# Converting the feed-forward weight to bf16 in 256 half-row transfers instead of 512 quarter-row ones, with a bf16 scratch tile

## The reference

```python
# attention, 16 heads of 64
q, k, v = rope(ln(x) @ wq.T), rope(ln(x) @ wk.T), ln(x) @ wv.T
scores = q k^T / 8 + slope_h * (key position - query position), causal
x = x + softmax(scores) @ v @ out_w.T + out_b
# feed-forward
xr = ln(x).reshape(b, t, 64, 16)
y = einsum('btri,hrij->bthrj', xr, rail_maker)      # 4 heads, 64 rails of 16
z = einsum('bthrj,hrkj->bthrk', y, rail_up_proj)    # 16384 columns
x = x + gelu(z.reshape(b, t, 16384)) @ w_cproj.T    # w_cproj is (1024, 16384)
```

## Time and profile before

| What | us |
|---|---|
| median of two runs | 3660.29 (3616.95 and 3703.63) |
| the profiled execution | 3630.47 |
| its span, slowest core (core 0) | 3628.9 |
| spans of the eight cores | 3590.0 to 3628.9 |
| PE busy | 2168.0 (60%) |
| ACT busy | 1058.1 (29%) |
| DVE busy | 770.3 (21%) |
| POOL busy, with its transfer issues | 372.6 (10%) |

### The profile page before, as it was taken

One profiled execution on the slowest core, in us unless ns is written; L12 is line 12 of the kernel. 1 busy time (PEld: TensorE's weight loads), 2 busy tenths in 40 slices (PEclk: granted clock), 3 DMA queues, 4 the chain that ended last, 5 costly groups with the idle time before them and its releaser, 6 DMA issues.

```text
span 3628.9 us, 34661 instructions; the slowest of 8 cores (3590.0 to 3628.9 us)
## 1 busy us (share of the span) xinstructions
PE 2168.0 (60%) x8094; PEld 862.7 (24%) x8094; DVE 770.3 (21%) x1803; ACT 1058.1 (29%) x1967; POOL 372.6 (10%) x705
## 2 busy tenths in 40 slices
PE   1268107426556665653000399759897887988989
PEld 0023002101111211211000122214343443434434
DVE  3300772224444444442000022200000000000000
ACT  1312111025445555552000011153232332333320
POOL 0022000122222222222222100000000000000000
PEclk9999557555666667675555555559998999999999
DMA  1122001353333333333333322238898888988888
GB/s 40 53 29 24 6 0 12 42 83 54 55 53 55 54 55 53 54 54 53 55 53 54 71 73 73 67 100 262 253 277 247 258 275 255 281 267 255 284 278 278
DMA packets 392162, 439.65 MB, mean 121 GB/s; under 512 B 63264, under 2 KB 247584, under 8 KB 391968
## 3 DMA queue, kind: packets, MB, share of 16 engines
q1 hardware_dynamic: 282368, 365.03, 33.5%
q0 software_dynamic: 98080, 47.23, 11.7%
q10 hardware_dynamic: 11520, 25.17, 1.8%
HBM read 425.73 MB, written 58.72 MB: 133 GB/s over the span
## 4 chain that ended last, share of the span: by engine, by line
DMA 44%; PE 33%; issue 9%; DVE 6%; ACT 4%; SPq 2%; POOL 1%; DVEq 0%; POOLq 0%; ACTq 0%
DMA wcv<-wcT 19%; PE pf L1047 17%; DMA wcb<-wcv 11%; DMA wcs<-wcb 11%; PE pat L902 6%; PE pqk L380 3%; PE pf L997 3%; PE pqk L494 2%; DMA bbuf<-blkB 2%; SPq L975 1%; DMA w2b<-w2scr 1%; DVE scrW L427 1%; SPq L991 1%; ACT sqd L254 1%; DVE lnst L248 1%
## 5 line engine op out<-in xcount | busy, mean ns | idle before, releaser
L1047 PE MATMUL pf<-wcs,Hb 128*128 128x512 bf16 x4096 | 1012.2, 385 | 156.8 <-DMA wcs<-wcb 155.1
L1010 ACT ACTIVATE Hb<-pf 128x256 bf16<-128x256 f32 x1024 | 394.4, 385 | 735.4 <-PE pf L997 710.2
L1047 PEld LDWEIGHTS pf<-wcs,Hb 128*128 128x128 bf16 x4096 | 393.9, 99 | 588.2 <-issue 230.8
L676 PE MATMUL ps<-qstg,KT 128*128 128x512 bf16 x559 | 308.7, 554 | 255.6 <-DVE qstg L668 219.6
L902 PE MATMUL pat<-owt,Ost 64*128 64x512 bf16 x512 | 224.1, 629 | 376.2 <-issue 376.2
L594 POOL DMA_DIRECT2D wcv<-wcT x512 | 271.3, 530 | 985.0 <-DMA wcb<-wcv 948.3
L753 PE MATMUL po<-pbuf,Vx 128*65 128x512 bf16 x559 | 309.5, 555 | 98.3 <-DVE Ost L812 80.5
L997 PE MATMUL pf<-btb,w2b 128*128 128x256 bf16 x1024 | 288.0, 289 | 43.6 <-DMA w2b<-w2scr 15.2
L1064 DVE TENSOR_TENSOR ob<-pf,xr 128x512 f32<-128x512 f32 x32 | 22.1, 692 | 1250.9 <-PE pf L997 891.1
L718 ACT ACTIVATE ebuf<-ps,cpool 128x512 bf16<-128x512 f32 x303 | 208.9, 689 | 88.3 <-PE ps L676 58.1
L711 ACT ACTIVATE ebuf<-ps,cpool 128x1024 bf16<-128x1024 f32 x128 | 142.9, 1116 | 281.3 <-PE ps L676 261.1
(11 more groups left out here) (99 smaller groups left out, 1335.3 us busy)
## 6 DMA issues: line engine op xcount, KB each, us to landing
wcs<-wcb SPq DMA_DIRECT2D x1024, 256.0 KB, 5.0
wcv<-wcT POOLq DMA_DIRECT2D x512, 64.0 KB, 2.6
wcb<-wcv SPq DMA_DIRECT2D x512, 64.0 KB, 1.5
w2b<-w2scr SPq DMA_DIRECT2D x256, 128.0 KB, 3.7
xin<-x SPq DMA_DIRECT2D x16, 512.0 KB, 4.2
xrb<-x SPq DMA_DIRECT2D x16, 512.0 KB, 5.1
xres<-xnw ACTq DMA_DIRECT2D x16, 512.0 KB, 5.3
xr<-xres SPq DMA_DIRECT2D x16, 512.0 KB, 6.7
```

Source lines behind the costliest of these rows:

```text
L676: P.op("tensor", (lambda p_=pr, f_=hf, kc_=kc, hc_=hc, qp_=qc % 2: (lambda e: e.matmul(ps[p_][:, 512 * f_:512 * (f_ + 1)], KT[0:128, S * h ...
L1010: P.op("scalar", (lambda m_=mc, z_=zb, p_=p: (lambda e: e.activation(Hb2[p_][:, SB2 * m_:SB2 * (m_ + 1)], pf[z_][:, 0:SB2], AF.Gelu, bias= ...
L1047: P.op("tensor", (lambda m_=mc, s_=sl2, e_=e2, pi=pb_i, i_=i, p_=p: (lambda e: e.matmul(pf[pi][:], Hb2[p_][:, SB2 * m_ + 128 * s_:SB2 * m_ ...
```

## The change

The conversion is cut in 256 rounds instead of 512. The two tiles `wcv` become [128, 512] instead of [128, 256], so a load fetches 2 KB of each of 128 rows instead of 1 KB, and a store writes 1 KB of each row instead of 512 bytes. The bytes in total, the two tiles, the two issuing engines and the waits between load and store are as before. The order of the instructions on all engines is as before too.

`sqd` becomes bf16. The sums of the exponentials stay float32 and no longer pass through it: DVE copies them straight into `rrow`, ACT's Ln works in place there, and the copy now also names `rrow_evt` among its waits.

```diff
-    sqd = es.enter_context(nc.sbuf_tensor("sqd", [128, 1024], F32))
+    sqd = es.enter_context(nc.sbuf_tensor("sqd", [128, 1024], BF16))
...
-    wcv = [p3_es.enter_context(nc.sbuf_tensor(f"wcv{i}", [128, D // 4], BF16, side="right"))
+    wcv = [p3_es.enter_context(nc.sbuf_tensor(f"wcv{i}", [128, D // 2], BF16, side="right"))
            for i in range(2)]
...
-    for mh in range(512):
-        mc, hh = divmod(mh, 4)
+    for mh in range(256):
+        mc, hh = divmod(mh, 2)
         i = mh % 2
         P.op("gpsimd", (lambda m_=mc, h_=hh, i_=i: (lambda e: e.dma_start(
-            out=wcv[i_][:], in_=wcT_d[128 * m_:128 * (m_ + 1), 256 * h_:256 * (h_ + 1)])))(),
+            out=wcv[i_][:], in_=wcT_d[128 * m_:128 * (m_ + 1), 512 * h_:512 * (h_ + 1)])))(),
              waits=[wcv_st[i]], inc=f"dcv{i}")
         wcv_ld[i] = P.now(f"dcv{i}")
         P.op("sync", (lambda m_=mc, h_=hh, i_=i: (lambda e: e.dma_start(
-            out=wcb_d[128 * m_:128 * (m_ + 1), 256 * h_:256 * (h_ + 1)], in_=wcv[i_][:])))(),
+            out=wcb_d[128 * m_:128 * (m_ + 1), 512 * h_:512 * (h_ + 1)], in_=wcv[i_][:])))(),
              waits=[wcv_ld[i]], inc=f"dcb{i}")
...
-    P.op("vector", lambda e: e.memset(sqd[64:66, :], 1.0), inc="v")
+    P.op("vector", lambda e: e.memset(rrow[64:66, :], 1.0), inc="v")
...
             P.op("vector", (lambda p_=pob: (lambda e: e.tensor_copy(
-                sqd[64:65, 512 * p_:512 * (p_ + 1)], po[p_][64:65, :])))(),
-                 waits=[ev_av, ev_vconst, drow_evt[pob]], inc="v")
+                rrow[64:65, 512 * p_:512 * (p_ + 1)], po[p_][64:65, :])))(),
+                 waits=[ev_av, ev_vconst, drow_evt[pob], rrow_evt[pob]], inc="v")
...
             rrow[64:66, 512 * p_:512 * (p_ + 1)],
-            sqd[64:66, 512 * p_:512 * (p_ + 1)],
+            rrow[64:66, 512 * p_:512 * (p_ + 1)],
             AF.Ln, bias=0.0, scale=1.0)))(),
```

## The result

The changed kernel takes 3270.2 us in the median of 11 runs (3251.0 to 3365.4), the kernel before 3637.5 us in 10 runs beside it (3610.7 to 3758.6). The ratio is 0.9013, with a 95% interval of 0.8971 to 0.9054. The profiled execution took 3270.2 us, with a span of 3268.7 us on core 3; the forecast was 3271.

What follows compares the result with a forecast made beforehand. Stage 3 was taken to be bound by the latency-limited weight conversion, ending 357.8 us after attention. Removing that hole gave 3628.9 - 357.8 = 3271.1 us, 3272.7 with 1.6 us around it; forecast 3271, range 3230 to 3350.

Steps and rivals of the forecast that it cites:

- The bound: Stage 3 lasts as long as the longer of attention (until 1682.6 us) and the conversion (until 2040.4 us).
- The price of a pair of rounds: Conversion: two half-row rounds take 5.7 us instead of 4.92, loads landing in 3.2 us and stores in 1.7.
- The median rows of bbuf and w2asm: Same-shape transfers elsewhere, 4.2 us a load and 3.0 a store, would give 8.0 us for a pair of rounds.
- the conversion later than attention: Stage 3: conversion stays the longer one, at 8.0 us a pair ending at 1804, time 3394 us; chance 0.10.
- the slower case: Conversion: 128 KB loads queue on one another, 10.7 us a pair, time 3740 us; chance 0.02.
- What was cut off: End of stage 3: of 530 us by which the conversion shrinks, 358 count, since attention then sets the end.
- Costs of nothing: Later stages, sums in rrow with their added wait, bf16 squares and more traffic beside attention: 0 us each.
- The sum: Core 0's span: 3628.9 - 357.8 = 3271.1 us, with the 1.6 us around it 3272.7.
- The way from attention's end to PE: Between attention and 3b: 16.6 us from POOL's first owT load to PE's first matmul, which stays.
- The clock rival: Output projection 3b: PE runs at 2.4 GHz instead of 1.2, saving 112 us, time 3160 us; chance 0.03.
- the rule cited in the prediction: TensorE clock: activity releases the throttle, so 3b should have risen already; the old trace disagreed, 0.50 beside 96% busy.

Runs made afterwards that it cites:

- the mixed kernel: Changed kernel with 64 row blocks of the weight converted in quarter rows and the other 64 in half rows: 3362.5 us.
- the two with quarter rows in two tiles: Changed kernel with the 512 quarter-row rounds put back, ratio 1.0007; kernel before with DVE's copy of the queries one job ahead, ratio 0.9996.
- Whole rows: Changed kernel with the conversion in 128 rounds of [128, 1024] instead of 256 half-row rounds: 3262.9 us.
- The packed kernels: Changed kernel with two heads side by side in Ost, 8 matmuls a group instead of 16: 3141.8 us; the same with owT loaded before the conversion: 3124.2 us.

## Why the prediction was right

*The bound.* The forecast rested on one reading, that stage 3 lasts as long as the longer of attention and conversion. It holds in every run: the conversion ends last where its last store is issued at 1776 us or later (the mixed kernel, the two with quarter rows in two tiles, the one with one tile), attention in all others, and the time follows to within 0.3% in the two where a late end of the conversion was worked out ahead (3366 for 3362.5 and 3750 for 3741.7).

*The price of a pair of rounds.* 5.7 us was forecast from the old transfers' own packet times, and 5.74 measured; the load landed in 3.2 us and the store in 1.7, both as forecast. The median rows of bbuf and w2asm, which gave 8.0, would have misled; they were taken beside other transfers, though no run shows that this is why. That rival, the conversion later than attention, is out, and with it the slower case. The hit on 5.7 is in part luck. A load's packets filled 34.5% of 720 us over 251 loads, 0.99 us on all engines against 0.57 for half the bytes, and a store's 0.39 against 0.23: together they grew by 0.57 us, where the prediction doubled them and added 0.80. The pair of rounds grew by 0.82 all the same, so 0.25 us of it is not in the packets, and what it is stays open. Whole rows, at 7.77 us, lie above the line through the two smaller sizes. The forecast hardly hung on it: any pair of half-row rounds below 7.05 us gives the same time.

*What was cut off.* Of 530 us by which the conversion was to shrink, 358 were to count. The conversion ended at 1508 (1510 forecast, from a start 9.1 us later), and PE's first matmul of 3b came 364.6 us earlier, of which 9.1 belong to the earlier start on this core.

*Costs of nothing.* The sums, the added wait and the squares: ratio 1.0007 without the rest. More traffic beside attention: 866.0, 866.4 and 866.0 us from the first multiplication to the last on core 1, with DMA shares of 0.33 (before), 0.49 (half rows) and 0.66 (whole rows) while the conversion ran. The stages behind: 3b took 281 us in both, and the feed-forward, from its first product with `wcb` (L1047) to its last, 1177 us on core 0 before and 1185 on core 3 after.

*The last microsecond is luck.* The sum was made for core 0 (3271.1), which came at 3252.3. The slowest is now core 3, which the same sum puts at 3241 (3590.0 less its own hole of 348.6) and which came at 3268.7. Over the eight cores the spans fell by 321 to 389 us, 359 in the mean, where the hole of core 0 was 357.8. Part of that spread is the feed-forward's: over the cores it took 1162 to 1178 us before and 1154 to 1186 after. The forecast also left out the 1.6 us that its own sum had added (3272.7).

*What the sum left out.* The way from attention's end to PE was to stay at 16.6 us and took 21.5, on the slowest core. POOL started 1.2 us later than the end of DVE's multiplication, and the owT loads landed in 9.5 us instead of 6.9. All eight cores now reach these loads within 10 us of each other (1667.8 to 1677.8; before 2011.5 to 2040.5), which could crowd them. But core 7 had 10.8 us before the change and 6.4 after it, so this is not shown. Loading owT early removes the wait, whatever its cause.

*The clock rival.* 3b stayed at 0.50, as forecast. The reason given was that the old 3b had not raised it in 280 us, so that a shorter standstill ahead of it would not either. The packed kernels fit this, with 0.78 in the first window both with a standstill of some 24 us and without it. They also show what the prediction did not ask: the stage can have a higher clock, once its matmuls contract 128 rows. Which property of them does it (the rows, their number, the gaps between them, in which PE waits for DVE and ACT) was not taken apart.

## What to carry to other kernels

When two independent streams meet at a barrier, work out the end of each before pricing an edit in either: the same copy moved ahead was worth 0.0% under the longer stream and 4% once that stream was shorter. A relay of small transfers through a few tiles is a cycle of latencies, so count bytes per cycle; twice the size or twice the tiles gave the same time here, and the packet time of the old transfer gave the cost of the larger one better (in part by luck) than the median of transfers of the new shape elsewhere. Make the hidden stream only as short as the other one needs, but look again after each gain on the visible one.

## What the runs showed of the hardware that was not expected

- The granted clock of TensorE did not follow its busy time alone (0.50 is 1.2 GHz): it stayed at 1.2 GHz for 280 us with PE busy for 28.93 of 30 us on 64-row matmuls, and stood at 0.72 to 0.84 of 2.4 GHz with PE busy for 20 to 23 of 30 us on 128-row ones in the same stage. By the rule cited in the prediction (the Trainium skill, TensorE: Matmul & The Clock Gate, section "What's actually happening"), activity releases the throttle; here the busier of the two stages stayed at 0.50, so these traces disagree with it if busy time is what counts as activity.
- One tile in flight took 5.33 us for a round, two tiles 5.74 us for two, four tiles of half the size 5.84 us for four: a second transfer in flight added 0.41 us to 5.33, and two more of the half size 0.92 us to 4.92. Two tiles of [128, 1024] took 7.77 us for two.
- A DVE product whose output lies 64 partitions above its inputs took at most 685 ns, the same as one in place (682 to 684).
